# Routed attention with its scores issued two heads at a time on two row halves, feed-forward weights rounded inside it, and the last three stages as one program

## The reference

```python
# routed attention, 8 heads of 64: a light branch over windows of 64 tokens with their neighbours ...
sim = einsum('bhnid,bhnjd->bhnij', qw * scale, kk); sim = where(valid, sim, neg)
attn = softmax(sim); lo = einsum('bhnij,bhnjd->bhnid', attn, vv); light_out = lo @ wo_l
# ... and a heavy branch: full attention among the 256 tokens with the largest routing scores
hattn = softmax(einsum('bhid,bhjd->bhij', hq * scale, hk)); ho = einsum(..., hattn, hv) @ wo_h
return light_out + zeros.at[iq].set(ho)
# full attention, 16 heads of 16, rotary embedding
# FP4 feed-forward: blocks of 16, scale = max|x| / 6, values rounded to the E2M1 grid
# h = silu(q(x) @ q(w_gate).T) * (q(x) @ q(w_up).T);  y = q(h) @ q(w_down).T
```

## Time and profile before

| | |
|---|---|
| median of 3 runs | 4453.76 us (4449.64 to 4458.86) |
| profiled execution, its own time | 4466.52 us |
| its span | 4464.7 us |
| PE busy | 3727.2 us, 83% of the span |
| DVE busy | 2867.2 us, 64% |
| ACT busy | 1911.5 us, 43% |
| POOL busy | 1574.8 us, 35% |
| granted clock of TensorE, mean | 0.92 |

### The profile page before, as it was taken

The page is one execution under the profiler, slowest core; times in us unless marked ns, Lnnn a source line. Parts: engine busy times, 40 slices in busy tenths (PEclk is TensorE's granted clock), DMA queues, the critical chain, the costliest instruction groups (busy, mean ns, idle before and its releaser), DMA issues. The chain is left out here.

```text
span 4464.7 us, 60005 instructions
## 1 busy us (share of the span) xinstructions
PE 3727.2 (83%) x19288; PEld 2571.7 (58%) x19288; DVE 2867.2 (64%) x5347; ACT 1911.5 (43%) x3864; POOL 1574.8 (35%) x1463
## 2 busy tenths in 40 slices
PE   5888877996799999987997688876885888888898
PEld 3455466885588888876786244444663333333566
DVE  5777555664555555455564577877884566664898
ACT  3556542432455545543442444422221455555222
POOL 4676535443665556435443111100002333330000
PEclk8899988998899999987999798897997699998999
DMA  5999712555000000002555000000002454450000
GB/s 137 275 288 238 237 39 88 161 161 160 10 17 14 11 10 11 1 30 82 156 161 173 24 12 17 19 1 15 0 0 51 87 103 80 97 101 15 9 10 19
DMA packets 221650, 348.36 MB, mean 78 GB/s; under 512 B 34632, under 2 KB 126266, under 8 KB 215226
## 3 DMA queue, kind: packets, MB, share of 16 engines
q1 hardware_dynamic: 198714, 260.66, 19.9%
q0 software_dynamic: 22656, 84.24, 8.3%
HBM read 166.29 MB, written 169.87 MB: 75 GB/s over the span
## 5 line engine op out<-in xcount | busy, mean ns | idle before, releaser
L2780 DVE TENSOR_REDUCE ab_nmx<-banks 128x1 f32<-128x512 f32 x512 | 334.7, 685 | 222.0 <-PE banks L2596 221.0
L1673 POOL TENSOR_TENSOR lb_pq<-lb_pq,lb_rr 128x512 f32<-128x512 f32 x192 | 204.4, 1068 | 308.0 <-DVE lb_rr L1552 305.0
L2722 ACT ACTIVATE ab_pt<-banks 128x512 f32<-128x512 f32 x512 | 273.8, 600 | 91.3 <-PE banks L2606 79.8
L2606 PE MATMUL banks<-ab_qT,ab_kT 49*128 49x512 f32 x512 | 231.6, 499 | 55.6 <-ACT ab_pt L2722 51.9
L1427 ACT ACTIVATE lb_pq<-banks,lb_nmx 128x256 f32<-128x256 f32 x384 | 178.9, 471 | 220.5 <-DVE lb_nmx L1547 217.4
L2596 PE MATMUL banks<-ab_kT,ab_qT 48*128 48x512 f32 x512 | 239.3, 515 | 31.2 <-DMA ab_kT<-ab_spill 19.1
L1547 DVE TENSOR_REDUCE lb_nmx<-banks 128x2 f32<-128x512 f32 x192 | 131.5, 685 | 186.0 <-PE banks L1279 185.0
L2606 PEld LDWEIGHTS banks<-ab_qT,ab_kT 49*128 49x128 f32 x512 | 93.8, 197 | 267.6 <-ACT ab_pt L2722 158.7
L358 ACT ACTIVATE da_pt<-banks 128x512 f32<-128x512 f32 (+1 forms) x384 | 179.1, 540 | 120.2 <-PE banks L270 116.4
L643 POOL DMA_INDIRECT mb_xi<-moe_ys,moe_b_place x64 | 63.5, 993 | 391.0 <-DVE mb_uT L2054 343.0
L285 PE MATMUL banks<-da_pt,da_vx 128*64 128x512 f32 (+3 forms) x1024 | 167.7, 473 | 29.9 <-POOL da_pt L577 26.1
(11 more groups left out here) (561 smaller groups left out, 11461.1 us busy)
## 6 DMA issues: line engine op xcount, KB each, us to landing
moe_xs<-zero SPq DMA_DIRECT2D x71, 512.0 KB, 11.5
moe_ys<-zero SPq DMA_DIRECT2D x71, 512.0 KB, 11.2
moe_a_w_raw<-in_moe_w SPq DMA_DIRECT2D x48, 512.0 KB, 4.7
moe_b_w_raw<-in_moe_w SPq DMA_DIRECT2D x48, 512.0 KB, 4.5
da_spill<-da_hi SPq DMA_DIRECT2D x128, 128.0 KB, 2.4
ab_spill<-ab_hi SPq DMA_DIRECT2D x128, 128.0 KB
da_qT<-da_spill POOLq DMA_DIRECT2D x32, 384.0 KB, 7.1
da_kT<-da_spill POOLq DMA_DIRECT2D x32, 384.0 KB, 10.7
```

The costliest lines, as they stand in the source:

```text
L1673: nc.gpsimd.tensor_tensor(pq[:, n % RING, :, :], pq[:, n % RING, :, :], bcast(rr[:, n % RING, :], 2, 2 * P), ALU.mult).then_inc(s_p, 1)
L2606: nc.tensor.matmul(ps[:, EXP_BANK + n % 3, :], kT[b % 2][r:r + AB_ROWS + 1, p, j * P:(j + 1) * P], qT[b % 2][r:r + AB_ROWS + 1, p, :], sta ...
L2722: nc.scalar.activation(pt[:, s % RING, :], ps[:, EXP_BANK + s % 3, :], ACT.Exp, scale=AB_D ** -0.5).then_inc(s_e, 1)
L2780: nc.vector.tensor_reduce(nmx[:, g % 2, col:col + 1], ps[:, MAX_BANK + n % 3, :], op=ALU.max, axis=AX.X, negate=True).then_inc(s_mx, 1)
```

## The change: what it does

Three parts.

1. Routed attention: queries are kept as 64 rows for each head, without the zeros. The scores of both slots of a pair are issued together in the even slot, alternating between rows 0-63 (bank 0) and rows 64-127 (bank 1). They wait for the exponentials of both slots of the pair before. DVE takes both maxima in the even slot.
2. The rounding of the feed-forward weights becomes 162 single DVE operations (18 pieces of 128 x 256 or 128 x 192, nine steps each), one in each of the slots 8 to 169 of routed attention. SP loads a piece, waits for its last step, stores it to DRAM, waits until it is stored, and loads the next. `fp4_weights` keeps only the transposes, and the weights are loaded from the rounded copy.
3. `fp4_ffn("f4a")`, full attention and `fp4_ffn("f4b")` are one block. Slots -90 to -39 of full attention are run between tiles 22 to 29 of the first feed-forward, the first jobs of the second feed-forward in slots `NS-34` to `NS-5` (`NS` is 512), and the last slots of full attention between tiles 0 to 7 of the second. The matmuls of gate and up use three banks (512, 192, 320 and 384 columns) and the output bank 3. The residual's scales for full attention are kept apart. The first feed-forward is unrolled for its tiles 20 to 31, the second for 0 to 9.

```diff
-def routed_attention(core, w, a, choice):
+def fp4_pieces(a, rounded):
+    pieces = []
+    for key in ("f4_wg", "f4_wu"):
+        for m in range(F4_IC):
+            pieces.append((a[key][m * P:(m + 1) * P, :], rounded[key][m * P:(m + 1) * P, :], C))
+    for c in range(KC):
+        for c0 in range(0, F4_I, C):
+            n = min(C, F4_I - c0)
+            pieces.append((a["f4_wd"][c * P:(c + 1) * P, c0:c0 + n], rounded["f4_wd"][c * P:(c + 1) * P, c0:c0 + n], n))
+    return pieces
...
+def routed_attention(core, w, a, choice, rounded):
...
+    pieces = fp4_pieces(a, rounded)
...
+    for i in range(9 * len(pieces)):
+        vector_jobs.setdefault(i + 8, []).append(("round", 0, i))
...
+                for n, (src, dst, size) in enumerate(pieces):
+                    if n:
+                        sp.wait_ge(s_fout, 16 * n)
+                    sp.dma_start(fx[:, 0, 0:size], src).then_inc(s_fin, 16)
+                    sp.wait_ge(s_fq, n + 1)
+                    sp.dma_start(dst, fx[:, 0, 0:size]).then_inc(s_fout, 16)
+                sp.wait_ge(s_fout, 16 * len(pieces))
...
                 def scores(n):
-                    b, m, kind, i, par = of(n)
+                    b, m, kind, i, _ = of(n)
                     c = (LB_FC * b + m) % 2
-                    bank = ps[:, S_BANK + n % 2, :]
                     if n >= 2:
-                        pe.wait_ge(s_e, n - 1)
+                        pe.wait_ge(s_e, n)
                     if kind == "light":
-                        if i == par == 0:
+                        if i == 0:
                             pe.wait_ge(s_qk, 2 * (LB_FC * b + m) + 2)
-                        nc.tensor.matmul(bank, identb[:, :], maskb[:, i, :], start=True, stop=False)
-                    elif par == 0:
+                        for par in range(2):
+                            nc.tensor.matmul(ps[:, S_BANK + par, :], identb[:, :], maskb[:, i, :], start=True, stop=False)
+                    else:
                         pe.wait_ge(s_hqk, LB_FC * b + m + 1)
                     for t in range(2):
-                        part = bank[:, 2 * P * t:2 * P * t + 2 * P]
                         qt = 2 * i + t
-                        if kind == "light":
-                            mine = q[:, c, par, qt * P:qt * P + P]
-                            keys = k[:, c, qt * P:qt * P + 2 * P]
-                        else:
-                            mine = hq[:, c, par, t * P:t * P + P]
-                            keys = hk[:, c, :]
-                        last = nc.tensor.matmul(part, mine, keys, start=(kind == "heavy"), stop=(kind == "heavy" or t == 1))
-                    last.then_inc(s_s, 1)
+                        for par in range(2):
+                            r = slice(LB_D * par, LB_D * par + LB_D)
+                            if kind == "light":
+                                mine = q[r, c, qt * P:qt * P + P]
+                                keys = k[r, c, qt * P:qt * P + 2 * P]
+                            else:
+                                mine = hq[r, c, t * P:t * P + P]
+                                keys = hk[r, c, :]
+                            last = nc.tensor.matmul(ps[:, S_BANK + par, 2 * P * t:2 * P * t + 2 * P], mine, keys,
+                                                    start=(kind == "heavy"), stop=(kind == "heavy" or t == 1))
+                            if t == 1:
+                                last.then_inc(s_s, 1)
...
-                    if 0 <= s + 2 < NS:
+                    if 0 <= s + 2 < NS and s % 2 == 0:
                         scores(s + 2)
...
-                            nc.scalar.copy(q[0:LB_D, chunk % 2, 0, :], bank[0:LB_D, :])
-                            nc.scalar.copy(q[LB_D:P, chunk % 2, 1, :], bank[LB_D:P, :]).then_inc(s_qk, 1)
+                            nc.scalar.copy(q[:, chunk % 2, :], bank).then_inc(s_qk, 1)
...
-                        nc.scalar.copy(hq[0:LB_D, chunk % 2, 0, :], bank[0:LB_D, 0:LB_SEL])
-                        nc.scalar.copy(hq[LB_D:P, chunk % 2, 1, :], bank[LB_D:P, 0:LB_SEL])
+                        nc.scalar.copy(hq[:, chunk % 2, :], bank[:, 0:LB_SEL])
...
+                def round_weights(b, i):
+                    n = i // 9
+                    size = pieces[n][2]
+                    x, v, m = (t[:, :, 0:size] for t in (fx, fv, fm))
+                    sc, inv = (t[:, 0:size // F4_BLK] for t in (fsc, finv))
+                    dve.drain()
+                    if i % 9 == 0:
+                        dve.wait_ge(s_fin, 16 * (n + 1))
+                    done = fp4_step(core, i % 9, x, sc, inv, v, m)
+                    if i % 9 == 8:
+                        done.then_inc(s_fq, 1)
...
-                for x in (q, hq):
-                    nc.vector.memset(x[LB_D:P, :, 0, :], 0.0)
-                    nc.vector.memset(x[0:LB_D, :, 1, :], 0.0)
...
-                    if 0 <= s + 2 < NS:
+                    if 0 <= s + 2 < NS and s % 2 == 0:
                         maxima(s + 2)
+                        maxima(s + 3)
...
-            @block.vector
-            def _(dve):
-                dve.wait_ge(core.loaded["f4"], core.loads["f4"])
-                for key, _ in kinds:
...
-                    fp4_round(core, dve, x, sc[:, 0:k], inv[:, 0:k], view(av), view(q)).then_inc(s_q, 1)
...
+                pe.wait_ge(core.loaded["f4"], core.loads["f4"])
                 for k, (key, _) in enumerate(kinds):
-                    pe.wait_ge(s_q, k + 1)
...
-def fp4_ffn(core, w, tag, store=None):
...
+class FeedForward:
...
+    def every_tile(self, eng, step, head, tail, beside):
+        for t in range(head):
+            step(t, t % 2)
+            beside(t)
+        with eng.Fori(head // 2, (F4_TILES - tail) // 2) as i:
             for k in range(2):
...
...
+        for key, c0, size, bank, at in (("f4_gT", 0, 512, 0, 0), ("f4_gT", 512, 192, 1, 0),
+                                        ("f4_uT", 0, 320, 1, 192), ("f4_uT", 320, 384, 2, 0)):
+            for c in range(KC):
+                last = nc.tensor.matmul(ps[:, bank, at:at + size], self.xT[:, k, c, :], w[key][:, c, c0:c0 + size],
+                                        start=(c == 0), stop=(c == KC - 1))
+        last.then_inc(self.s_gu, 1)
...
+AB_EARLY = 5
...
+    odd[NS - 24], odd[NS - 20] = ("fx", 0, 0), ("fx", 0, 1)
...
+                    if s == NS - 16:
+                        pe.wait_ge(s_mx, NS)
+                        last_ffn.gate_up(pe, 0, 0)
+                    if s == NS - 5:
+                        last_ffn.gate_up(pe, 1, 1)
...
+                    if s == NS - 34:
+                        act.wait_ge(s_rows, B - 1)
+                        last_ffn.roots(act, 0, B - 1)
+                    if s == NS - 31:
+                        act.wait_ge(last_ffn.s_shift, 1)
+                        last_ffn.normalised(act, 0, 0)
+                        last_ffn.normalised(act, 1, 1)
+                    if s == NS - 10:
+                        last_ffn.normalised(act, 2, 0)
+                    if s == NS - 12:
+                        last_ffn.silu(act, 0, 0)
...
+                    if s == NS - 33:
+                        last_ffn.scales(dve, 0, B - 1, 1)
+                        last_ffn.pads(dve)
+                    if s in (NS - 30, NS - 26):
+                        last_ffn.rounded_x(dve, (s - NS + 30) // 4)
+                    if s == NS - 11:
+                        last_ffn.product(dve, 0, 0)
...
+def last_stages(core, w, x, store):
...
+    head = {22: (-90, -88), 23: (-88, -86), 24: (-86, -84), 25: (-84, -76), 27: (-76, -58), 28: (-58, -38)}
+    head_vector = {26: (-90, -70), 27: (-70, -60), 29: (-60, -38)}
+    with own, ctx:
+        tiles, stacked = [], []
+        for i in range(2):
+            with ExitStack() as space:
+                tiles.append(FeedForward.tiles(core, space, f"f4{i}_"))
+            stacked.append([ctx.enter_context(nc.sbuf_tensor(f"ab_{n}T{i}", [P, AB_H // 2, T], F32R)) for n in "qk"])
+        f1 = FeedForward(core, w, ctx, own, "f4a", tiles[1], False)
+        f2 = FeedForward(core, w, ctx, own, "f4b", tiles[0], True)
+        att = full_attention(core, w, x, ctx, own, stacked, f1, f2)
+        NS = att.NS
+        end = {0: (NS + 3, NS + 8), 2: (NS + 8, NS + 11), 3: (NS + 11, NS + 13), 4: (NS + 13, NS + 16),
+               6: (NS + 16, att.last_slot)}
+        end_vector = {t + 1: slots for t, slots in end.items()}
+        with nc.Block() as block:
+            @block.sync
+            def _(sp):
...
+            @block.tensor
+            def _(pe):
+                def beside_first(t):
+                    if t in head:
+                        att.pe(pe, *head[t])
+                def beside_last(t):
+                    if t in end:
+                        att.pe(pe, *end[t])
+                    if t == 8:
+                        pe.wait_ge(att.s_rows, B)
+                for t in range(2):
+                    f1.turn_x(pe, t, t)
```

(69 more changed lines are left out.)

501 lines of the change are left out of this document (256 added, 245 removed).

## The result

| | before | after |
|---|---|---|
| median | 4456.0 us (4449.6 to 4458.9, 4 runs) | 4387.7 us (4382.4 to 4400.5, 4 runs) |
| ratio, 95% interval | | 0.9855 (0.9833 to 0.9878) |
| span of the profiled execution | 4464.7 us | 4383.3 us |

The change makes the kernel 65 to 68 us faster (1.45%). The forecast was 4325, with a range of 4275 to 4380: the direction was right, the gain was half of what was said, and the time lies 8 us above the range.

A forecast was written before the change was run, and what follows sets the result against it. PE was taken to bound routed attention (busy 737.6 of 746 us), with idle stretches at the borders. Terms of -25, -30.5, -45 and -28 made -128.5 from 4466.5, 4338; less 12.7 for the median, 4325, range 4275 to 4380.

The forecast's parts named there:

- the wait for both banks: Routed attention: PE's scores of a pair wait for both previous slots' exponentials; +38 us, ends 0 and 85.
- The second border: Full attention into second feed-forward: 43.8 us go, 22.7 are added, 6 more saved; taken as -28, ends -15 and -38.
- The overlap: Routed attention: score matmuls on two row halves run fully side by side; -83 us.
- the mode change: Routed attention: each pair enters and leaves the halved form, PE losing 0.09 us each time; +18 us, ends 0 and 33.
- Rounding in stage three: Routed attention: DVE's added weight rounding and its DMA waits are mostly hidden; +4 us, 31 without cover.
- B: Routed attention: waits twice as long, through DVE's rounding, `rank` and ACT's exponentials; 4373 us; chance 0.16 with E's mild form.
- The rounding stage: `fp4_weights`, before the first feed-forward: only bursts on PE and ACT stay, 39.6 us become 9; -30.5 us.
- The first border: First feed-forward into full attention: first maxima follow the last statistics after 2.9 instead of 48.6 us; -45, ends -30 and -55.
- E's mild form: Routed attention: short waits in every pair bring PE's mean clock to 0.93; 48 us, 4373; chance 0.16 with B.
- D: Both borders pay half, since each engine's queue waits at the seam for the slowest; +36 us, 4361; chance 0.13.
- A: Routed attention: the wait for both banks costs nothing, the stage gives 65 less 4 us; 4289; chance 0.2.
- C: Routed attention: row halves don't run side by side for products with two records; +83, -38, 4370 us; chance 0.05.

The follow-up runs named there:

- pairs alone: Kernel before, with a pair's scores issued together and waiting for both exponentials, 128 rows and zeros kept: ratio 1.0181, first to last exponential of routed attention 834.1 us.
- the roots moved: Changed kernel, with ACT's three square roots of each routed-attention batch behind the exponentials of slot 5 instead of ahead: ratio 0.9780.
- part 1 alone: Kernel before with only the paired scores on row halves, no rounding in routed attention, old borders: ratio 1.0039, first to last exponential 765.9 us.
- part 1 with the roots moved: Kernel before with only the paired scores on row halves, and the square roots behind the exponentials: ratio 0.9951, first to last exponential 731.7 us.
- the early exponentials: Changed kernel, with ACT taking the exponentials of both slots of every routed-attention pair in the even slot: ratio 0.9771.
- the best kernel: Changed kernel, square roots behind the exponentials, and both exponentials of a pair in the even slot only in slot 14 and the last batch: ratio 0.9747, 4333.5 us.

## Why the prediction was wrong, step by step

The step that failed is the wait for both banks, +38 in the sum: it left the roots and their two table loads out of ACT's queue, and these cost 33 us. The second border gave 20 us less than forecast, 11 of them in slots that the sum did not touch.

The profile's span fell by 81.4 us where 128.5 were forecast: 47 of the 63 us between forecast and median. Some 15 more are the step from profile to median: I took 12.7 us off, as in the kernel before, but here the median lies 2.5 above the profiled execution. In the order of time, by the rows above:

| | forecast | measured |
|---|---|---|
| start of the first exponentials of routed attention | -2 | -8.4 |
| stage three | -23 | +18.0 |
| last exponential to the last statistics before `fp4_weights` | 0 | -4.3 |
| from there to the first rounding of the feed-forward | -30.5 | -32.6 |
| from there to the first exponential of full attention | -45 | -46.1 |
| full attention's exponentials and all that follows | -28 | -8.0 |

(The -2 for the memsets belongs in the first row. Of its -8.4, 7.2 lie ahead of the first instruction of routed attention, 1094.04 before and 1086.87 after, and the -4.3 in experts and state space: the change touches neither, and over the fourteen traces the one instruction starts between 1083.7 and 1094.0 and the other stretch takes 1077 to 1089 us. The last row is +32.7 for the slots and -40.7 behind them.)

- **The wait for both banks failed.** It was forecast at +38 with an upper end of 85; pairs alone measured +83. My list of waits went slot by slot through ACT's copies, and left out ACT's other table: the roots in slot 3 with two table loads. For that slot pair I had 0.27 us and it was 3.2, with the lower clock behind it, 33 us in seven batches. Slot 15's 2.0 was right (1.7 in the changed kernel, 2.0 with the roots moved). With the roots out of the way stage three with part 1 alone is 19.5 shorter, where the same terms gave -83 + 18 + 38 = -27.
- **The overlap held, its price did not.** The groups of the scores took 82 us less of PE (194.2 to 112.3) where I had 83. Net of the mode change -65 was forecast; 68 measured by time, 65 by PE's busy time, some 8 of it clock. Inside it the mode change was too cheap: the loader is idle 0.75 us a pair at the two changes, where I had 2 x 0.17; by the same share of it that is an estimate of 38 us in place of 18. That would be most of why PE's busy time fell by 39, not by 65, once the clock was even (part 1 with the roots moved).
- **Rounding in stage three held** (+4 against +3.7), the DMA waits being 12.6 us on a DVE with cover. The 3.7 is little more than executions of one routed attention differ by: 751.2 and 753.4 with the roots' place alone changed, 769.2 to 773.9 in three kernels with that of the change. What I wrote under B, that rounding would make the waits twice as long, was wrong in its cause: the waits were longer, but not by DVE. Its sum was wrong too: +38 + 20 is 58, and I priced it at 48.
- **The rounding stage** gave 32.6, not 30.5: what is left of it takes 7.0 us (3005.86 to 3012.81) where I had 9. The other 4.3 of the 37 come before it.
- **The first border held** as a sum (-46.1 against -45), which is luck in part: two errors cancel, with the feed-forward 8.5 us longer (3021.37 to 3379.90 is 358.5, against 350.0) where I had 1.5, and 54.6 less from the last statistics to the first exponential where I had 48.6. (My terms add up to -47.1; I wrote -46 and took -45.)
- **The second border** was forecast at -28. By the tail and what follows it, it gave -18.7 (+22.0 and -40.7). The tail's +22.0 is near the 22.7 that I had added, but by luck: some 11 of it are the lower clock, where I had 3 us of gain for a PE "kept warmer", and some of what I had added, as the end of batch 7, falls behind the tail. Of the 46.8 that were to go behind it (43.8, and 3 for the first tile's wait) 40.7 went.
- **The other 10.7 us** are in the exponentials of batches 0 to 6 (564.1 to 574.8), which the forecast did not touch. Batch 1 is 14 us longer by itself (batch 0 is 7 shorter); here it is after and before:

```profile
3491.00:3587.00 96.00, 86.38 (x349) 33.39 (x348) 50.96 (x88) 43.18 (x83) 30.64 (x37) 0.77 0.39 78
```

```profile
3571.00:3653.00 82.00, 71.75 (x350) 28.75 (x352) 50.87 (x89) 43.43 (x82) 31.04 (x38) 0.96 0.46 91
```

Seven other kernels with the new borders took 568 to 580 us for batches 0 to 6, five others with the old ones 554 to 566, so it is more than chance. It is the clock: length times mean clock is 525 to 531 us in all fourteen, 525.1 before (0.931) and 527.2 after (0.917), 528 in the mean for the old borders and for the new. What sets the clock there stays open.
- **The rivals.** B's price (+10 to +35 in stage three) came true, with another cause; E's mild form is in it (0.98, some 10 us). D came in part: the borders gave 54 of the 73 us. What is missing is missing at the second, and most of it is the clock, not the waits at the seam that D named. A and C did not come: with the early exponentials A is not reached either, since other waits take the place of the first.
- **The signs that I named** served in part. The waits on ACT's drain were there, but the longest came at the roots, not in the slot pair without an odd job. The clock stayed above the 0.97 that I had named (0.98). The window was 765 where I had named 700 to 730, and 730 for the best kernel.

The Trainium skill, TensorEngine Tiling (Array Packing), Key Properties, has the change of tiling mode as a drain of TensorE. The trace agrees with it: 0.41 and 0.34 us of idle loader at each change.

The Trainium skill, ScalarE: Activation LUTs, What ACT_TABLE_LOAD costs, gives about 2.66 us for a switch, half of it the load and half a drain. The trace agrees on the load (1.28) and shows no such drain: two loads with three roots between them take 3.19 us (1455.89 to 1459.08), where two of the page's switches alone would be an estimated 5.3. Here the measured number is the one to use.

## What to carry to other kernels

When two jobs that were issued a slot apart are joined, list everything that stands in the consumer's queue ahead of the second one (table loads too), since all of it now lies between the bank and its next use. Then move that work behind the consumer before judging the join: here two lines turned a loss of 17 us into a gain of about 20. And when a wait is removed by reordering, try it first only in the slots where it was long: done everywhere, it came back as waits for the copies that were put off. (The difference between the two was 4 us here, at the edge of what was measured.)
